# A mixture-of-experts decoder kernel: where the scatters of the routing weights stand on Pool's queue

## The chip, the core and the metric

The kernel runs on one core of one Trainium2 chip. The metric is the time of one launch on the device in microseconds. Engines are named TensorE (PE in the profile; PEld is its weight load), VectorE (DVE), ScalarE (ACT), GpSimd (POOL) and SyncE (SP). "SPq" and "POOLq" are the instructions by which an engine only issues a transfer or takes part in a barrier.

## The reference

Two decoder layers over x of 16 x 128 x 512, float32 throughout. Each has self attention, cross attention and a feed-forward part, and a layer norm after each. What matters here is the last part, a mixture of experts:

```python
logits = x @ gate_weight.T                       # 8 experts
scores = softmax(logits); topk_w, topk_idx = top_k(scores, 2)
combine = zeros((T, E)).at[arange(T)[:, None], topk_idx].add(topk_w)
gu = einsum('th,efh->tef', x, gate_up_weights)
act = silu(gu[..., :F]) * gu[..., F:]
y = einsum('tef,te,ehf->th', act, combine, down_weights)
...
y = y + (silu(sgu[:, :Fs]) * sgu[:, Fs:]) @ shared_down.T
x = layernorm(x + y)
```

T is 2048 tokens, F is 352, and the shared part that every token goes through is 704 wide.

## The kernel before

The program is a row of phases, one after the other: the attention "gqa", a latent cross attention, a ternary feed-forward part, the attentions "decay" and "causal", then the shared part of the mixture (`shared_ffn_phase`) and its experts (`expert_ffn_phase`). A phase is a block of five instruction streams, one for each engine. At its end all engines meet in a barrier, clear the phase's semaphores (L175 to L199), meet in a second one and start the next phase together.

X, the 2048 tokens by 512, stays in the on-chip memory as 16 tiles of 128 tokens. The shared phase does two things at once. TensorE multiplies the tokens by the shared weights in two halves, s = 0 and s = 1. For each group of four tiles and each of the weights' parts j it makes the products gate and up (`ups`), VectorE multiplies them (L1804, `hf`), ScalarE and VectorE split the result into a high and a low part (L1658 `hh`, L1789 `hl`), and TensorE makes the down product of it (`down`). After the last part of a group, VectorE adds the sums to that group's tiles of X (`sums`, L1783). That happens four times in each half.

Beside this the tokens are sorted by expert. VectorE works out for every token and each of its two experts a row number, `S.pos` (the last step is L1751), and the routing weight of each, `S.score`. The rows lie in 39 tiles of 128 slots in the device's memory. Pool then writes X's rows to `x_slots` (L1621: one indirect transfer for each tile t and each k of the two experts, 128 rows of 2 KB) and the routing weights to `s_slots` (L1628: 128 numbers of 4 bytes each). The expert phase loads them tile by tile: `x_slots` as input, `s_slots` as a factor at L1967.

What sets the order around the change: Pool issues in the order of its code. After every fourth tile it waits until all X scatters so far have landed (semaphore `scattered`, 16 for each). In the s = 0 half `sums` changes X, so it waits for `scattered` too: group g must have left before VectorE adds to it. TensorE's next down product that starts a bank anew waits for `sums` (`y_free`). SyncE loads three blocks of weights in this phase. The third (L1610, the first expert's) waits for VectorE's last split of the block before it (L1682), and `first_x` (L1612) waits for all of `scattered`. The scores have a semaphore of their own, `scored`; nobody but Pool waits for it, and the loads of `s_slots` come after the barrier.

```python
                if t % GT == GT - 1:
                    pool.wait_ge(scattered, 16 * 2 * (t + 1))
...
                if n and n % 2 == 0:
                    pool.wait_ge(scored, 16 * n)
...
                        if s == 0:
                            dve.wait_ge(scattered, m * (2 * 16 * 2 * GT) + (gg + 1) * 16 * 2 * GT)
```

Of the kernel before, what the change touches and what calls it, by code (L numbers as in the profile page):

```python
# [12 lines left out]
B = 16  # L13
# [143 lines left out]
class Phase:  # L157
# [11 lines left out]
    def sem(self, name):  # L169
        self.sems.append(self.ctx.enter_context(self.nc.semaphore(f"{self.name}_{name}")))  # L170
        return self.sems[-1]
# [1342 lines left out]
def shared_ffn_phase(nc, S, w):  # L1514
# [13 lines left out]
    with Phase(nc, "shared") as phase:  # L1528
# [26 lines left out]
        slots_done, rows_done, scattered, scored = sem("slots_done"), sem("rows_done"), sem("scattered"), sem("scored")  # L1555
# [46 lines left out]
        @block.sync  # L1602
        def _(sp):
            sp.dma_start(gw[:, :, :], w["router"]).then_inc(gw_in, 16)
            sp.dma_start(route[:, :], w["route"]).then_inc(route_in, 16)
            sp.dma_start(raw[:, :], w["experts"][E * P:(E + 1) * P, :]).then_inc(raw_in, 16)
            sp.wait_ge(w_lo, A_DONE)
            sp.dma_start(raw[:, :], w["experts"][(E + 1) * P:(E + 2) * P, :]).then_inc(raw_in, 16)
            sp.wait_ge(w_lo, B_DONE)
            sp.dma_start(raw[:, :], w["experts"][0:P, :]).then_inc(raw_in, 16)  # L1610
            sp.wait_ge(scattered, 16 * 2 * B)
            sp.dma_start(S.first_x[:, :], S.x_slots[0:P, :]).then_inc(first_x_in, 16)  # L1612
            sp.wait_ge(first_x_in, 16)

        @block.gpsimd
        def _(pool):
            pool.wait_ge(slots_done, 1)
            for t in range(B):
                for k in range(2):
                    at = bass.IndirectOffsetOnAxis(ap=S.pos[:, k * B + t:k * B + t + 1], axis=0)  # L1620
                    pool.indirect_dma_start(S.x_slots, at, S.X[:, t, :], None).then_inc(scattered, 16)  # L1621
                if t % GT == GT - 1:
                    pool.wait_ge(scattered, 16 * 2 * (t + 1))
            for n in range(2 * B):
                at = bass.IndirectOffsetOnAxis(ap=S.pos[:, n:n + 1], axis=0)
                if n and n % 2 == 0:
                    pool.wait_ge(scored, 16 * n)
                pool.indirect_dma_start(S.s_slots, at, S.score[:, n:n + 1], None).then_inc(scored, 16)  # L1628
            pool.wait_ge(scored, 16 * 2 * B)

        @block.scalar
# [183 lines left out]
        def _(pe):  # L1815
# [43 lines left out]
            def body(s, last):  # L1859
                for m in halves(pe, s):  # L1860
# [4 lines left out]
                    def down(q):  # L1865
                        j, r = q % J, rows_of(s, q)
                        pe.wait_ge(hl_done, t + (2 * Q * s + q + 1))
                        if s == 0 and m == 0 and q in (0, J - 1):
                            pe.wait_ge(w_lo, A_DONE if q == 0 else A_DONE + 1)


                        if j == 0 and q:
                            pe.wait_ge(y_free, m * (2 * GT) + (B * s + (q // J) * GT))
                        for i in range(GT):
                            cols = slice(i * P, (i + 1) * P)
                            for (at, high), (_, low) in zip(down_w(weh, s, j), down_w(wel, s, j)):
                                ins = products(pe, yb[i][:, at:at + high.shape[1]], hh[r, q % 2, cols], hl[r, q % 2, cols],
                                               high, low, j == 0, j == J - 1 and at + high.shape[1] == DM)
                            ins.then_inc(down_done, 1)
# [513 lines left out]
```

## Time and profile before

| | us |
|---|---|
| median of 3 runs | 2107.75 |
| lowest and highest | 2102.79, 2109.4 |
| the profiled execution | 2106.78 |
| its span in the trace | 2104.9 |

| engine | busy us | share of the span |
|---|---|---|
| PE | 1932.6 | 92% |
| PEld | 1575.4 | 75% |
| DVE | 1044.6 | 50% |
| ACT | 711.8 | 34% |
| POOL | 386.6 | 18% |

The causal attention ends at about 1550 us from the start of the span, the shared phase runs to 1791 and the expert phase to the end. A row of a timeline has the start, the length, the engine, the line, what it writes and reads, and in brackets how long the engine had stood idle and what ended that. A transfer's own row covers only its issue; "DMA to landing" counts from the start of the issue until its data is there. The granted clock is a share of TensorE's 2.4 GHz: 0.50 is 1.2 GHz.

### The profile page before, as it was taken

What the parts mean: (1) busy time and instruction counts of PE and PEld (TensorE: products, weight loads), DVE (VectorE), ACT (ScalarE), POOL (GpSimd) and SP (SyncE); (2) the same over time, 40 slices, a digit from 0 to 9 for tenths busy, and PEclk for the clock granted to TensorE, in tenths of its full rate; (3) what the DMA queues carried; (4) which work ended last, traced back from release to release, by engine and by line L of the source; (5) the groups of instructions that cost most, each with busy time, mean ns of one, the idle gap of its engine ahead of it and who ended that gap; (6) DMA issues with size and microseconds to landing.
All of it is one profiled execution on the core that took longest, in us unless ns stands there. A gap on an engine that the chain in (4) does not pass through costs nothing. (4 is left out here: it accounts for less than half of the span.)

```text
span 2104.9 us, 32789 instructions
## 1 busy us (share of the span) xinstructions
PE 1932.6 (92%) x12124; PEld 1575.4 (75%) x12124; DVE 1044.6 (50%) x1836; ACT 711.8 (34%) x2275; POOL 386.6 (18%) x339
## 2 busy tenths in 40 slices
PE   8999888999999979999899999899979996999991
PEld 6777677788888757877678877677758874899990
DVE  5676753455555455333455556676755232222224
ACT  4555634344444422212221112444632211233332
POOL 2110100000000056000021100000104222644335
PEclk9999999999999989999999999999999998999995
DMA  7211051000000021000290001000015100644257
GB/s 236 59 42 42 1 193 47 1 1 1 1 1 1 1 106 60 0 0 0 92 388 6 1 31 41 1 1 1 2 46 185 66 0 0 240 136 154 80 112 204
DMA packets 73376, 135.89 MB, mean 65 GB/s; under 512 B 13457, under 2 KB 31761, under 8 KB 71185
## 3 DMA queue, kind: packets, MB, share of 16 engines
q1 hardware_dynamic: 47376, 96.28, 13.2%
q0 software_dynamic: 7888, 27.94, 4.5%
q10 hardware_dynamic: 17968, 9.71, 1.8%
q8 instruction: 96, 1.57, 0.3%
q14 instruction: 48, 0.39, 0.1%
HBM read 90.62 MB, written 43.29 MB: 64 GB/s over the span
## 5 line engine op out<-in xcount | busy, mean ns | idle before, releaser
L1470 PE MATMUL banks<-ternary_xth,ternary_wq 128*128 (+1 forms) x352 | 141.0, 401 | 5.3 <-DVE ternary_wq L1401 3.9
L1470 PE MATMUL banks<-ternary_xtl,ternary_wq 128*128 (+1 forms) x352 | 139.4, 396 | 0.0
L571 ACT ACTIVATE causal_pr<-banks,causal_nb 128x128 f32<-128x128 f32 x256 | 89.9, 381 | 52.3 <-DVE causal_nb L713 52.3
L97 PE MATMUL banks<-latent_vh,latent_cth 128*128 128x512 f32 x256 | 104.2, 407 | 3.5 <-DVE latent_ctl L1171 3.5
L97 PE MATMUL banks<-weights,expert_xgh 128*128 x312 | 104.8, 336 | 2.4 <-DVE expert_xgl L2083 2.4
L571 ACT ACTIVATE gqa_pr<-banks,gqa_nb 128x128 f32<-128x128 f32 x256 | 89.9, 382 | 45.5 <-DVE gqa_nb L713 45.5
L99 PE MATMUL banks<-weights,expert_xgl 128*128 x312 | 101.5, 325 | 0.0
L98 PE MATMUL banks<-weights,expert_xgh 128*128 x312 | 101.5, 325 | 0.0
L99 PE MATMUL banks<-latent_vh,latent_ctl 128*128 128x512 f32 x256 | 100.2, 391 | 0.0
L98 PE MATMUL banks<-latent_vl,latent_cth 128*128 128x512 f32 x256 | 100.1, 391 | 0.0
L1430 DVE TENSOR_TENSOR ternary_hf<-ternary_sg,banks 128x512 f32<-128x512 f32 x44 | 30.2, 687 | 135.5 <-issue 79.6
L1124 ACT ACTIVATE latent_pt<-banks 128x1024 f32<-128x1024 f32 x32 | 32.9, 1027 | 187.9 <-PE banks L1270 187.9
L1371 ACT ACTIVATE ternary_sg<-banks 128x512 f32<-128x512 f32 x44 | 26.3, 598 | 192.8 <-PE banks L1470 192.8
L1115 ACT ACTIVATE latent_pr<-banks,latent_nb 128x128 f32<-128x128 f32 x256 | 90.0, 372 | 0.0
L1085 POOL TENSOR_TENSOR latent_rs<-latent_ve,mhalf 128x1 f32<-128x1 f32 x15 | 8.2, 549 | 444.3 <-DVE latent_ve L219 444.3
L97 PE MATMUL banks<-latent_xgh,latent_ch 128*128 128x256 f32 x256 | 77.2, 302 | 9.4 <-DVE latent_xgl L1165 4.6
L1470 PEld LDWEIGHTS banks<-ternary_xth,ternary_wq 128*128 128x128 f32 x352 | 67.4, 192 | 23.6 <-DVE ternary_xtl L70 4.2
L1482 PE MATMUL banks<-ternary_wq,ternary_hh 128*128 128x512 f32 x176 | 71.0, 403 | 8.1 <-DVE ternary_hl L1434 5.8
L1171 DVE TENSOR_TENSOR latent_ctl<-banks,latent_cth 128x512 fp32r<-128x512 f32 x64 | 42.8, 689 | 71.6 <-ACT latent_cth L1102 71.6
L1470 PEld LDWEIGHTS banks<-ternary_xtl,ternary_wq 128*128 128x128 f32 x352 | 67.4, 191 | 14.3
L743 DVE TENSOR_TENSOR X<-X,banks 128x512 f32<-128x512 f32 x48 | 33.0, 687 | 81.4 <-PE banks L99 81.4
L2091 DVE TENSOR_TENSOR expert_hf<-expert_sg,banks 128x352 f32<-128x352 f32 x39 | 20.3, 521 | 105.4 <-PE banks L99 105.4
(462 smaller groups left out, 5538.4 us busy)
## 6 DMA issues: line engine op xcount, KB each, us to landing
x_slots<-decay_zeros SPq DMA_DIRECT2D x39, 256.0 KB, 4.6
y_slots<-decay_zeros SPq DMA_DIRECT2D x39, 256.0 KB, 4.9
y_slots<-expert_ys SPq DMA_DIRECT2D x39, 256.0 KB, 2.1
expert_xin<-x_slots SPq DMA_DIRECT2D x38, 256.0 KB, 2.9
weights_raw<-in_expert_experts SPq DMA_DIRECT2D x4, 2176.0 KB, 9.7
gqa_tw<-in_ternary_w ACTq DMA_DIRECT2D x4, 2112.0 KB, 10.7
ternary_raw<-in_ternary_w SPq DMA_DIRECT2D x11, 768.0 KB, 4.1
expert_raw<-in_expert_experts POOLq DMA_DIRECT2D x3, 2176.0 KB, 10.0
```

The source lines that it names most:

```text
L97: pe.matmul(out, wh, xh, start=first, stop=False, **kw)
L98: pe.matmul(out, wh, xl, start=False, stop=False, **kw)
L99: return pe.matmul(out, wl, xh, start=False, stop=last, **kw)
L571: a = act.activation(pr[:, h, c, :], S.bank[2 * h + c // 4][:, (c % 4) * P:(c % 4 + 1) * P], ACT.Exp, bias=nb[:, h, c:c + 1], accum_out=su ...
L743: dve.tensor_tensor(row, row, bank, ALU.add).then_inc(free_d, 1)
L1115: a = act.activation(pr[:, c, :], S.bank[x][:, j * P:(j + 1) * P], ACT.Exp, bias=nb[:, c:c + 1], accum_out=sums[:, c:c + 1])
L1124: act.activation(pt[:, :, :], pair(1), ACT.Copy).then_inc(pt_done, 1)
L1171: dve.tensor_tensor(ctl[:, x, :], S.bank[2 + x], f32(cth[:, x, :]), ALU.subtract).then_inc(ct_lo, 1)
L1371: act.activation(sg[:, j % 2, :], gate[j % 2][:, :], ACT.Sigmoid).then_inc(sig_done, 1)
L1430: dve.tensor_tensor(hf[:, j % 2, :], sg[:, j % 2, :], up[j % 2][:, :], ALU.mult).then_inc(hf_done, 1)
L1470: a = pe.matmul(dst[:, :], wq[:, j, m, c * P:(c + 1) * P], x[:, c, toks], start=c == 0 and n == 0, stop=c == C - 1 and n == 1)
L1482: a = pe.matmul(yb[i][:, :], h[:, j % 2, i * P:(i + 1) * P], wq[:, j, 2, :], start=j == 0 and n == 0, stop=j == J - 1 and n == 1)
```

## The change

The loop over the scores is taken apart: each tile's two score scatters stand right behind that tile's two X scatters. The wait after every second score scatter is gone; there is one wait for all 32 at the end, as before. Pool's wait for the X rows after every fourth tile stays, and stands behind that tile's score scatters.

```diff
                 for k in range(2):
                     at = bass.IndirectOffsetOnAxis(ap=S.pos[:, k * B + t:k * B + t + 1], axis=0)
                     pool.indirect_dma_start(S.x_slots, at, S.X[:, t, :], None).then_inc(scattered, 16)
+                for k in range(2):
+                    n = k * B + t
+                    at = bass.IndirectOffsetOnAxis(ap=S.pos[:, n:n + 1], axis=0)
+                    pool.indirect_dma_start(S.s_slots, at, S.score[:, n:n + 1], None).then_inc(scored, 16)
                 if t % GT == GT - 1:
                     pool.wait_ge(scattered, 16 * 2 * (t + 1))
-            for n in range(2 * B):
-                at = bass.IndirectOffsetOnAxis(ap=S.pos[:, n:n + 1], axis=0)
-                if n and n % 2 == 0:
-                    pool.wait_ge(scored, 16 * n)
-                pool.indirect_dma_start(S.s_slots, at, S.score[:, n:n + 1], None).then_inc(scored, 16)
             pool.wait_ge(scored, 16 * 2 * B)
```

No other engine's instructions change. On Pool, the start of the phase (L1615 is its first instruction there), with - for before and + for now. The names in brackets are the semaphores' first users; here latent_kvr_in is `slots_done`, latent_late_chain is `scattered` and latent_late_rs is `scored`:

```order
 L1615 UNCONDITIONAL_BRANCH [waits barrier_Pool_Activation_PE_DVE_SP_gather]
 L1621 DMA x_slots<-X,pos 4992x512 [waits latent_kvr_in]
-L1621 DMA x_slots<-X,pos 4992x512 x7
+L1621 DMA x_slots<-X,pos 4992x512
+L1625 DMA s_slots<-score,pos 4992x1 x2
+L1621 DMA x_slots<-X,pos 4992x512 x2
+L1625 DMA s_slots<-score,pos 4992x1 x2
+L1621 DMA x_slots<-X,pos 4992x512 x2
+L1625 DMA s_slots<-score,pos 4992x1 x2
+L1621 DMA x_slots<-X,pos 4992x512 x2
+L1625 DMA s_slots<-score,pos 4992x1 x2
 L1621 DMA x_slots<-X,pos 4992x512 [waits latent_late_chain]
```

Tile 3's second X scatter, on which the first `sums` waits, was the 8th transfer of the phase and is the 14th.

The end of Pool's stream in this phase, before (a pair with its wait, sixteen times in all, then the wait for the last) and now:

```order
184 L1628 DMA s_slots<-score,pos 4992x1 [waits latent_late_rs]
185 L1628 DMA s_slots<-score,pos 4992x1
186 L1628 DMA s_slots<-score,pos 4992x1 [waits latent_late_rs]
187 L1628 DMA s_slots<-score,pos 4992x1
188 L1910 UNCONDITIONAL_BRANCH [waits latent_late_rs]
```

```order
179 L1625 DMA s_slots<-score,pos 4992x1 x2
180 L1621 DMA x_slots<-X,pos 4992x512 x2
181 L1625 DMA s_slots<-score,pos 4992x1 x2
182 L1621 DMA x_slots<-X,pos 4992x512 x2
183 L1625 DMA s_slots<-score,pos 4992x1 x2
184 L1909 UNCONDITIONAL_BRANCH [waits latent_late_rs,latent_late_chain]
```

The score scatters keep their number and their data; no wait stands between them any more.

## Rows read from the trace of the kernel before

**Rows 1.** The waits, 1700 to 1792: engine, line waited for, total, times, longest.
```profile
PE banks L2143 <- PEq L175: 21.3, 1, 21.3
```

**Rows 2.** The timeline of all engines, 1769.5 to 1792.2, end of the phase.
```profile
1769.17 1.37 DVE L1783 TENSOR_TENSOR X<-X,banks 128x512 f32 x2
1769.30 0.39 PE L99 MATMUL banks<-weights,shared_hl 64*128 64x512 f32 x1
...
1790.98 0.10 POOL L1990 MEMSET expert_spare<- 128x1 f32 x1 [11.27 <-POOLq L175]
...
1791.02 1.09 PE L2143 MATMUL banks<-ident,first_x 128*128 128x128 f32 x4 [21.33 <-PEq L175]
```

**Rows 3.** Line 1628: ns min/median/max, first and last start; landing times.
```profile
L1628 POOL DMA_INDIRECT s_slots<-score,pos x32: 952/957/4297, 1647.8 to 1778.8; - x32
...
DMA to landing us min/median/max: 2.5/5.9/8.5
```

**Rows 4.** Pool's timeline, 1602 to 1609.
```profile
1602.32 0.96 POOL L1621 DMA_INDIRECT x_slots<-X,pos  x1 [0.30 <-issue]
...
1607.88 2.12 POOL L1621 DMA_INDIRECT x_slots<-X,pos  x1 [0.30 <-issue]
```

**Rows 5.** The timeline of all engines, 1549 to 1552, the boundary before.
```profile
1549.41 0.55 DVE L622 TENSOR_SCALAR X<-X,causal_mv,causal_rs 128x512 f32<-128x512 f32 x1 [0.66 <-POOL causal_rs L481]
1551.84 0.33 SPq L1604 DMA_DIRECT2D shared_hf<-in_expert_router  x1
```

**Rows 6.** Line 1621: all 32, then the three issued from 1625.4.
```profile
L1621 POOL DMA_INDIRECT x_slots<-X,pos x32: 954/960/2117, 1593.1 to 1644.8; - x32
...
DMA to landing us min/median/max: 2.7/2.7/9.5
...
L1621 POOL DMA_INDIRECT x_slots<-X,pos x3: 958/961/962, 1625.4 to 1627.9; - x3
...
DMA to landing us min/median/max: 7.4/7.8/8.0
```

**Rows 7.** Line 1628: the second pair of score scatters, then the last.
```profile
L1628 POOL DMA_INDIRECT s_slots<-score,pos x2: 957/958/958, 1658.0 to 1659.2; - x2
...
DMA to landing us min/median/max: 4.7/6.0/7.2
...
L1628 POOL DMA_INDIRECT s_slots<-score,pos x2: 954/956/957, 1777.5 to 1778.8; - x2
...
DMA to landing us min/median/max: 4.9/5.2/5.4
```

**Rows 8.** VectorE's timeline, 1560 to 1700: the four sums of s = 0.
```profile
1609.68 2.47 DVE L1783 TENSOR_TENSOR X<-X,banks 128x512 f32<-128x512 f32 x4
...
1624.73 2.78 DVE L1783 TENSOR_TENSOR X<-X,banks 128x512 f32<-128x512 f32 x4 [1.15 <-PE banks L99]
...
1656.10 2.47 DVE L1783 TENSOR_TENSOR X<-X,banks 128x512 f32<-128x512 f32 x4
...
1674.05 2.78 DVE L1783 TENSOR_TENSOR X<-X,banks 128x512 f32<-128x512 f32 x4 [1.37 <-PE banks L99]
1682.82 4.69 DVE L1682 TENSOR_TENSOR weights<-weights_raw,weights 128x4352 fp32r<-128x4352 f32 x1 [5.99 <-ACT weights L1647]
```

**Rows 9.** TensorE's timeline: first instruction of three down products.
```profile
1612.30 0.47 PE L97 MATMUL banks<-weights,shared_hh 128*128 128x512 f32 x1
...
1637.53 0.39 PE L97 MATMUL banks<-weights,shared_hh 128*128 128x512 f32 x1
...
1689.56 0.65 PE L97 MATMUL banks<-weights,shared_hh 128*128 128x512 f32 x1 [2.55 <-DVE shared_hl L1789]
```

**Rows 10.** TensorE in two stretches: us, busy, PEclk, DMA share, GB/s.
```profile
1690.00:1694.00 4.00, 4.00 (x13) 0.60 0.01 0
...
1794.00:1799.00 5.00, 5.00 (x18) 0.50 0.91 297
```

**Rows 11.** SyncE's timeline, 1622 to 1624: the first expert's weights.
```profile
1623.01 0.33 SPq L1610 DMA_DIRECT2D weights_raw<-in_expert_experts  x1
```

## The prediction

> **What bounds the kernel now.** Read first the waits between 1700 us and 1792 us: TensorE, which is busy almost everywhere else, stands idle for 21.3 us at one place, ahead of the first transpose of the expert phase (L2143) [rows 1]. The timeline of that place says who is late. TensorE's last product of the shared phase starts at 1769.30, VectorE's last two additions into X run from 1769.17 to 1770.54, and then nobody works but Pool: its last two score scatters are issued at 1777.5 and 1778.8 and land 4.9 and 5.4 us later, the second at 1784.2 [rows 7], and all engines start the next phase together at 1790.98 to 1791.02 [rows 2]. A phase ends with a barrier that all engines must reach. So the end of this phase is Pool's, not TensorE's, by about 20 us. Pool is that late because of line 1628. The group of that line shows 32 scatters with a median of 0.957 us each, first start 1647.8, last 1778.8, each landing a median of 5.9 us after its issue [rows 3]: 131 us for about 31 us of issuing, the rest is the wait after every second one, that the new code doesn't have.
>
> **What is removed.** Without the waits Pool's own work is 64 issues. Their pitch is 1.26 us (from the first, 1593.1, to the eighth, 1602.32, are 9.2 us, less 0.4 us for a slow start, so 8.8 over seven steps) [rows 4, 6]. 64 x 1.26 = 81 us, to 1674; with the waits for rows that are counted below, some ten microseconds more, about 1685. The last score lands at most 8.5 us later [rows 3], so before 1694. That is 76 us ahead of VectorE's last addition: all that Pool still has at the end is hidden by the s = 1 half of TensorE's products (L97 to L99), and if that cover were shorter by 76 us, Pool would be the end again.
>
> What ends the phase then? VectorE at 1770.54. The price of a boundary whose last work is VectorE's is read at the one before this phase: the last addition there runs from 1549.41 for 0.55, and SyncE's first issue of the next phase is at 1551.84 [rows 5]: 1.88 us. With it the expert phase starts at 1770.54 + 1.88 = 1772.4 and not 1790.98, a gain of **18.6 us** if nothing in the shared phase moves. It takes in the 6.8 us between the last score's landing (1784.2) and 1790.98, of which 1.9 are the boundary and 4.9 are something that follows Pool's own last scatter; Pool would now have that 70 us early, so I count all of it.
>
> **What is moved, and what waits for it.** X is scattered from the same rows that VectorE adds into later (sums, L1783), so sums waits for `scattered`, four tiles at a time, and TensorE's next down product waits for sums (y_free). Putting two score scatters behind each tile doubles the distance between tiles. Four times it can matter:
>
> Group 1 (tiles 0 to 3). The last X scatter was the 8th issue, 1602.32; it is now the 14th: 6 x 1.26 = 7.6 us later, 1609.9. One issue of that stretch, at 1607.88, took 2.12 us instead of 0.96 [rows 4]; I keep these 1.2 us, since it falls in the same time: 1611.1. An X scatter alone lands after 2.7 us [rows 6], so 1613.8. But the score scatters of tile 2 were issued just before. Those of the second pair landed after 4.7 and 7.2 us (issued 1658.0 and 1659.2) and those of the last after 4.9 and 5.4 [rows 7]. If X's count must come in behind them it is 1614 to 1616. I take 1615. sums began at 1609.68 with four additions in 2.47 us, and TensorE's down product that reads their bank began at 1612.30, right after [rows 8, 9]. Here is no slack: 1615 + 2.5 + 0.15 = 1617.7, a stall of **5.4** us (4.0 if X lands after its 2.7).
> A stall has a second price. After the 2.55 us of idle at 1689.56 the granted clock was 0.60 over 1690 to 1694 [rows 9, 10]: one stretch of about 3.4 us at 1.2 instead of 2.4 GHz, 1.7 us lost. I add **1.7** once. The shift is now 7.1.
>
> Group 2 (tiles 4 to 7). Pool's 17th issue starts at 1593.1 + 16 x 1.26 + 1.6 = 1614.9, a little after X has landed, so about 1615.3; tile 7's second X scatter is 13 issues on, 1631.7, with half a microsecond for another slow issue 1632. In the kernel before it was issued at 1627.9, beside the load of a whole expert's weights that SyncE issued at 1623.01, and the three last ones needed 7.4 to 8.0 us to land [rows 6, 11]. That load waits for VectorE's line 1682, which is now behind the late sums, so it moves along by the same 5 us and still covers 1632. Landing at 1640. sums (2.8) to 1642.8, then hf, ACT's hh and hl of about 0.7 each: 1645.0. Before, sums stood at 1624.73 and TensorE's down product at 1637.53; sums, hf, hh and hl need 5.0 us of that, so there was some 8 us of room [rows 8, 9]. TensorE goes on at 1645.0 instead of 1637.53: a shift of 7.5, **0.4** more than it brings along.
>
> Groups 3 and 4. Pool goes on at 1640.3, tile 11's rows are issued by 1656.7 and land by 1663; sums needs them at 1656.10 + 7.5 = 1663.6. Tile 15's: 17th issue after that at 1660.6, so 1677.1 and 1683; needed at 1674.05 + 7.5 = 1681.6, and behind that sums VectorE had 5.99 us of idle before line 1682 [rows 8]. Both fit: **0**.
>
> **The queue itself** is what the trace can't show, since no X scatter stands behind a score scatter in it. From one side: no cost beyond a single landing (X after 2.7). From the other: score scatters are served one behind the other. In the two pairs of [rows 7] the second landed 3.8 and 1.8 us after the first, though issued 1.3 apart, so a scatter may hold the queue for 1.8 to 3.8 us, with a middle of 2.8, and a tile for 5.6, against 5.05 us of issuing. That is near enough to even that I count only the short delay above.
> The Trainium skill, DMA: Bandwidth & Descriptors, Queues, rings and completion order, says that a transfer's semaphore count is a strongly ordered write that lands only after every earlier write of the same DMA engine. By that rule X always lands behind the scores ahead of it; no row here shows it. By it the stall in group 1 would be near its 1616 end, without it near 1613.8.
>
> **Clock behind the boundary.** Before, the granted clock was 0.50 over 1794 to 1799 although TensorE was busy for all 5.00 us [rows 10]. The idle time ahead is now under 3 us and not 21. Between nothing and half of those 5 us comes back; I take **0.9**.
>
> **Sum.** 18.6 - 5.4 - 1.7 - 0.4 + 0.9 = 12.0 us. The profiled execution took 2106.78 (span 2104.9), so 2094.8; on the median of the runs, 2107.75, it is **2095.8**. The load of the weights, the tiles of x_slots and Pool's work of the expert phase all start from the boundary and move with it.
>
> **Rivals.** (a) X doesn't queue behind scores: stall 4.0 in group 1, tile 7 after 2.7 us and so no second stall, 18.6 - 4.0 - (0 to 1.7) + 0.9 = 14 to 15.5, about 2093. For it: an X scatter's landing is flat at 2.7 us wherever nothing large is under way. Against it: scores land more slowly than X, though they carry 4 bytes a row and X 2 KB. Chance 0.17.
> (b) **Slower: the queue is the limit.** Served strictly in turn, a tile costs two scores at 2.8 to 3.8 and two X scatters of about 0.7. Tile 15's rows land at 1593 + 4 + 15 x pace. They are needed at 1674 + 6; the gain of 18.6 is gone when they land after 1698.6, so the point is a pace of **6.8** us a tile. At 5.6 + 1.4 = 7.0 it is about 3 us slower than before; at 3.3 a scatter (8.0 a tile) tile 15 lands at 1717, TensorE ends 37 us late, and the time is 2107.75 + 18.4 = 2126. Of this speaks for it that the pair takes 8.65 us from issue to issue (129.7 us over 15 pairs, from 1647.8 to 1777.5) [rows 3, 7]; against it that a part of that is plain latency, which overlaps. Slower by over 0.3%: 0.08.
> The Trainium skill, same page, Specifications, says that transfers under 512 bytes are done by read-modify-write; it would make (b) likelier, since every score is 4 bytes. The trace agrees so far as 5.9 us against 2.7 go.
> (c) Between: some queueing, two or three stalls, a shift of 13 to 24 us where I have 7.5. Gain from 6 down to a loss of 5, 2102 to 2112, most of it within 0.3%. Chance 0.17 with the mild half of (b).
> (d) Pool's tail of 4.9 us is a price of the boundary and not of Pool's last scatter: gain 7 us, 2101. The boundary of [rows 5] speaks against it. Chance 0.05.
>
> **Chances.** 0.3% (6.3 us) is about what a measurement can tell from no change. Forecast 0.53 (gain 8 to 15), (a) 0.17, (d) 0.05, (c) 0.17, (b) 0.08. Faster by over 0.3%: 0.53 + 0.17 + some of (d) = 0.73; within 0.3%: 0.19; slower 0.08. The range goes from (a) with no stall at all (2107.75 - 18.6 - 1.5 = 2087.6) to no gain, 2107.
>
> **What the profile of after would show.** TensorE's wait at L2143 down from 21.3 to under 3 us; Pool's last issue before 1700; all starts at about 1780. X scatters with a median landing above 2.7 us if they queue. In sums one wait for x_slots of about 5 us at 1610 and one at 1632. It would be wrong if Pool's issues of group 4 run far past 1685, which is (b), or if TensorE has no idle near 1612, which is (a) or better.

## The result, and the profile after

| | before | after |
|---|---|---|
| median us | 2106.11 (4 runs) | 2125.07 (4 runs) |
| lowest and highest | 2102.79, 2109.4 | 2121.66, 2127.38 |
| the profiled execution | 2106.78 | 2123.46 |
| its span | 2104.9 | 2121.7 |

The changed kernel is **slower**: 1.0079 times the time of before, 95% interval 1.0061 to 1.0097. The forecast was 2095.8 us, and its range ended at 2107.0.

In this execution the sort gave Pool its row numbers 2.1 us later than in the one of before (Pool's first issue at 1595.2 instead of 1593.1 [rows 6]); every time below holds these 2.1 us.

The end of the phase, in the waits between 1750 and 1812 (engine, line, total, times, longest), and in the timeline. The row of L2142 answers to the wait of [rows 1], all three of the timeline to [rows 2]:

```profile
POOL expert_spare L1989 <- POOLq L175: 105.6, 1, 105.6
```
```profile
1805.96 0.39 PE L99 MATMUL banks<-weights,shared_hl 64*128 64x512 f32 x1
1808.50 0.10 POOL L1989 MEMSET expert_spare<- 128x1 f32 x1 [105.56 <-POOLq L175]
1808.54 1.08 PE L2142 MATMUL banks<-ident,first_x 128*128 128x128 f32 x4 [2.19 <-PEq L175]
```

The wait of 21.3 us is gone: TensorE stands idle for 2.19 us between the phases, and Pool is there 105 us ahead. But the expert phase starts at 1808.50, where it started at 1790.98. TensorE's last product, at 1769.30 before, comes at 1805.96.

Where TensorE lost that is plain from two windows, from the sort's end to TensorE's last product of the phase, of before and then of after (stretch, its length, busy us and matmuls, granted clock, share of the DMA engines, GB/s):

```profile
1593.00:1769.70 176.70, 173.63 (x793) 0.99 0.17 62
```
```profile
1595.10:1806.30 211.20, 181.34 (x793) 0.92 0.25 52
```

The same 793 matmuls take 34.5 us longer: 26.8 us more idle time (29.9 against 3.1) and 7.7 us more busy time, at a clock of 0.92 instead of 0.99 (the mean over the stretch, stalls included). Against that stand 19.1 us from the boundary (21.33 to 2.19). With the start 2.1 us later this is the 17.5 us by which the expert phase starts late.

The waits of after between 1597 and 1720 say who was waited for:

```profile
DVE X L1782 <- DMA x_slots<-X,pos: 29.5, 2, 18.9
DVE shared_hf L1803 <- remote: 24.7, 2, 13.8
POOL x_slots L1621 <- DMA x_slots<-X,pos: 24.3, 3, 13.9
...
PE banks L97 <- DVE X L1782: 10.3, 1, 10.3
```

and VectorE's timeline shows the four `sums` (L1782 now; [rows 8] before) and the third place at which TensorE stood:

```profile
1622.12 2.48 DVE L1782 TENSOR_TENSOR X<-X,banks 128x512 f32<-128x512 f32 x4 [10.62 <-DMA x_slots<-X,pos]
1657.62 2.48 DVE L1782 TENSOR_TENSOR X<-X,banks 128x512 f32<-128x512 f32 x4 [18.92 <-DMA x_slots<-X,pos]
1683.58 2.47 DVE L1782 TENSOR_TENSOR X<-X,banks 128x512 f32<-128x512 f32 x4
1705.80 0.69 DVE L1803 TENSOR_TENSOR shared_hf<-shared_sg,banks 128x512 f32<-128x512 f32 x1 [13.79 <-remote]
1709.69 0.69 DVE L1782 TENSOR_TENSOR X<-X,banks 128x512 f32<-128x512 f32 x1 [1.81 <-PE banks L99]
```

TensorE's down products behind these, which answer to [rows 9]:

```profile
1624.75 0.77 PE L97 MATMUL banks<-weights,shared_hh 128*128 128x512 f32 x1 [10.25 <-DVE X L1782]
1662.14 0.80 PE L97 MATMUL banks<-weights,shared_hh 128*128 128x512 f32 x1 [9.34 <-DVE shared_hl L1788]
1707.93 0.58 PE L97 MATMUL banks<-weights,shared_hh 128*128 128x256 f32 x1 [7.22 <-DVE shared_hl L1788]
```

Three stalls, 26.8 us. Each is followed by a stretch at half clock (PEclk is the third number from the end, in front of the DMA share and GB/s):

```profile
1624.70:1630.40 5.70, 5.65 (x13) 4.47 (x14) 2.60 (x3) 0.63 (x1) 4.29 (x5) 0.50 0.25 92
1662.00:1668.00 6.00, 5.86 (x14) 4.60 (x15) 1.38 (x3) 0.63 (x1) 4.76 (x5) 0.50 0.30 89
1707.90:1712.30 4.40, 4.37 (x20) 4.37 (x21) 1.50 (x3) 0.00 (x0) 0.00 (x0) 0.50 0.26 42
```

Half of 5.65, 5.86 and 4.37 is 7.9 us: the busy time that was added (7.7) to within 0.2.

Why the rows are late is on Pool's queue. The last X scatter of group 1 and the first one behind the wait for that group, then the same of group 2, in the timeline of Pool:

```profile
1613.30 0.96 POOL L1621 DMA_INDIRECT x_slots<-X,pos  x1 [0.30 <-issue]
...
1622.37 0.95 POOL L1621 DMA_INDIRECT x_slots<-X,pos  x1 [5.58 <-DMA x_slots<-X,pos]
...
1640.50 0.96 POOL L1621 DMA_INDIRECT x_slots<-X,pos  x1 [0.30 <-issue]
...
1657.87 0.95 POOL L1621 DMA_INDIRECT x_slots<-X,pos  x1 [13.88 <-DMA x_slots<-X,pos]
```

Tile 3's rows are there 8.8 us after their issue (sums starts at 1622.12), tile 7's 17.1 us. Beside it runs the load of the first expert's weights, which answers to [rows 11]; line 1610 of after:

```profile
L1610 SPq DMA_DIRECT2D weights_raw<-in_expert_experts x1: 327/327/327, 1638.1 to 1638.1; - x1
...
DMA to landing us min/median/max: 18.2/18.2/18.2
```

It took 10.2 us before, and the rows issued beside it needed some 8 us then [rows 6], not 2.7. Single landings of the scatters themselves are mostly missing from this trace, so those of [rows 3, 6, 7] have no counterpart in it; the times above are those at which the waiting engines went on.

### The profile page after: what moved, and what is told of

Its sections match the earlier page's. It is cut to its first block and busy times, and to the rows that moved or that the text cites. A ratio compares the mean times of both kernels' runs of the same rounds, so it can differ in the third digit from the quotient of the medians.

```text
span 2121.7 us, 32790 instructions
## 1 busy us (share of the span) xinstructions
PE 1941.6 (92%) x12124; PEld 1583.6 (75%) x12124; DVE 1043.1 (49%) x1836; ACT 711.6 (34%) x2275; POOL 384.6 (18%) x339
## 5 line engine op out<-in xcount | busy, mean ns | idle before, releaser
L98 PE MATMUL banks<-latent_xgl,latent_ch 128*128 128x256 f32 x256 | 72.9, 285 | 0.0
L99 PE MATMUL banks<-latent_xgh,latent_cl 128*128 128x256 f32 x256 | 72.8, 285 | 0.0
```

The costliest lines, as they stand in the source:

```text
L98: pe.matmul(out, wh, xl, start=False, stop=False, **kw)
L99: return pe.matmul(out, wl, xh, start=False, stop=last, **kw)
```

## Does the boundary give what was expected?

Every ratio from here on is to the kernel before, run beside the kernel in question, and the brackets give its 95% interval. Two kernels leave the boundary's gain alone in view. The first keeps the order of before and takes only the waits between the scores away; the second is the changed kernel with its four lines of score scatters and their wait left out (the experts are then weighted by the zeroed slots).

```diff
             for n in range(2 * B):
                 at = bass.IndirectOffsetOnAxis(ap=S.pos[:, n:n + 1], axis=0)
-                if n and n % 2 == 0:
-                    pool.wait_ge(scored, 16 * n)
                 pool.indirect_dma_start(S.s_slots, at, S.score[:, n:n + 1], None).then_inc(scored, 16)
```

> The kernel before with one part of the change alone: the waits after every second score scatter are gone, but all 32 X scatters still stand first. Theory Q (X's counts land behind the scores ahead of them in the queue, a score scatter holds it about 2.8 us): no score is ahead of an X scatter, so the four sums start where they did (the first some 17 us after Pool's first scatter), Pool's last issue is near 1690, the last landing near 1740, and the shared phase ends with VectorE: 18.6 us less than before, about 2088. Rival R (a backlog of small writes delays TensorE's own signals, as at 1698 in the changed kernel, wherever it stands): the backlog of 90 us lies beside TensorE's work and costs stalls of several microseconds each, 2095 to 2110.

> The changed kernel without the 32 score scatters and their wait; the routing weights stay zero, so the experts' part of the output is left out, while the expert phase does the same work. Every theory: X scatters as in the kernel before, no stall, the phase ends with VectorE, about 2088. It measures the term of 18.6 us for the end of the phase by itself; if the tail of 4.9 us belongs to the boundary, 2093.

Measured: rows first without waits **2087.06** us (4 runs; ratio 0.9897, 0.9876 to 0.9919), without scores 2086.91 (4 runs; 0.9892, 0.9875 to 0.9909). The last product and the start of the next phase with the rows first, from the timeline, and its group of score scatters:

```profile
1769.29 0.38 PE L99 MATMUL banks<-weights,shared_hl 64*128 64x512 f32 x1
...
1771.83 0.10 POOL L1988 MEMSET expert_spare<- 128x1 f32 x1 [79.56 <-POOLq L175]
```
```profile
L1626 POOL DMA_INDIRECT s_slots<-score,pos x32: 954/958/5002, 1647.8 to 1691.1; - x32
...
DMA to landing us min/median/max: 5.0/7.0/9.3
```

TensorE ends where it did before (1769.30), and the next phase starts 19.1 us earlier than at 1790.98. So the removal of the waits is worth its 18.6 us, and the move of the scores is what costs. The group shows more: 32 scatters issued without a pause in 43 us land at most 9.3 us behind their issue, so they don't pile up; they are served at one in 1.4 us or less. A scatter that held it for the 2.8 us of the prediction would have left the last one some 45 us behind.

Whether the order among the scores matters (tile by tile, as the changed kernel has them, and not all of k = 0 first) was one kernel more:

```diff
-            for n in range(2 * B):
+            for m in range(2 * B):
+                n = (m % 2) * B + m // 2
```

> As the kernel with all X scatters first and no waits between the scores, but the scores go tile by tile (both experts of a tile, then the next tile), the order that they have in the changed kernel. Theory M (scores and X scatters hinder each other when mixed): the order among the scores does nothing, the last issue is near 1692 and the landings have a median of 6 to 9 us, as with the other order. Theory O (a tile's two score scatters meet at the same addresses, so this order is slow by itself): landings of 10 us and more, 32 scores need 2.7 us each, the last landing near 1735. Either way about 2088.

2087.95 us (one run), landings 4.5/6.9/9.5. It doesn't matter.

## What the score scatters do to the rows

All kernels of this section have the order of the changed one. In the first the score scatters carry rows of 2 KB to `y_slots` instead (the experts' weights are again the zeroed ones). In the second the score slots lie 256 bytes apart, and the loads read them with that stride:

```diff
-                    pool.indirect_dma_start(S.s_slots, at, S.score[:, n:n + 1], None).then_inc(scored, 16)
+                    pool.indirect_dma_start(S.y_slots, at, f32(xtl[:, 0, 0:DM]), None).then_inc(scored, 16)
```
```diff
-                    at = bass.IndirectOffsetOnAxis(ap=S.pos[:, n:n + 1], axis=0)
-                    pool.indirect_dma_start(S.s_slots, at, S.score[:, n:n + 1], None).then_inc(scored, 16)
+                    at = bass.IndirectOffsetOnAxis(ap=spos[:, n:n + 1], axis=0)
+                    pool.indirect_dma_start(S.s_slots.rearrange("a (b c) -> (a b) c", c=1), at, S.score[:, n:n + 1], None).then_inc(scored, 16)
...
+                dve.tensor_scalar(spos[:, :], posf[:, :, :].rearrange("p k t -> p (k t)"), float(64), None, ALU.mult).then_inc(slots_done, 1)
...
-        S.s_slots = nc.dram_tensor("s_slots", (SLOTS, 1), F32).ap()
+        S.s_slots = nc.dram_tensor("s_slots", (SLOTS, 64), F32).ap()
```

`spos` are the row numbers times the distance between slots, counted in numbers of 4 bytes.

> The changed kernel with each score scatter replaced by a scatter of 128 rows of 2 KB (from a tile that nobody changes, into y_slots, which is overwritten later), at the same place and with the same semaphore; the routing weights stay zero, so the experts' part of the output is left out. Theory Q: it is the 4-byte writes that hold the queue, so X lands 2.7 to 4 us after its issue, the first sums starts about 4 us late instead of 10, and the time is 2090 to 2096. Rival (the number and the place of the scatters, not their kind): X lands after 9 to 17 us and the time stays near 2125.

> The changed kernel with s_slots widened from 4 bytes a slot to 256, so that no two scores fall into the same 256 bytes; same scatters, same 4 bytes each, same order. VectorE makes a second list of row numbers (one more small instruction). Theory Q1 (writes of 4 bytes are slow because neighbours in memory take turns): a score scatter lands after 3 us, X after 3 to 4, time 2090 to 2096. Theory Q2 (each 4-byte write is slow wherever it goes): X lands as late as in the changed kernel and the time stays at 2120 to 2128.

Measured: 2099.39 us with 2 KB rows (4 runs; 0.9953, 0.9936 to 0.997), 2096.36 with the spread slots (4 runs; 0.9942, 0.9923 to 0.9962). The spread kernel's first two sums, its X scatters, and its score scatters:

```profile
1613.53 2.48 DVE L1787 TENSOR_TENSOR X<-X,banks 128x512 f32<-128x512 f32 x4 [4.53 <-DMA x_slots<-X,pos]
1639.68 2.48 DVE L1787 TENSOR_TENSOR X<-X,banks 128x512 f32<-128x512 f32 x4 [9.94 <-DMA x_slots<-X,pos]
```
```profile
L1625 POOL DMA_INDIRECT x_slots<-X,pos x32: 956/960/1232, 1592.7 to 1676.9; - x32
...
DMA to landing us min/median/max: 2.7/2.7/6.9
```
```profile
L1629 POOL DMA_INDIRECT s_slots<-score,shared_spos x32: 954/958/2292, 1595.5 to 1679.4; - x32
...
DMA to landing us min/median/max: 2.1/2.1/8.7
```

The spread kernel is what was forecast for the changed one, in its time and in its places: sums waits 4.5 us in group 1 and TensorE 4.2 us behind it, the rest is hidden. It has the same number of transfers, of the same 4 bytes, in the same order, and is 28.7 us faster. With 2 KB rows the time lies 3.4 us above what was expected (2090 to 2096), but far from the 2125 of the rival. So neither the number of small scatters nor their place on the queue makes the loss, but that the numbers are written next to one another: row numbers are given out expert by expert in the order of the tokens, so the 128 numbers of a scatter fall on a few short runs of neighbouring slots. Scatters of 512 times the data hurt far less, if they go to rows of their own. Why neighbouring writes are slow, no run here shows.

How far apart must the slots be? Three kernels keep the order and the waits of before and only send the scores into an array of their own, with 8192, 8448, 16 and 64 bytes from slot to slot (it isn't read; the experts are weighted by zeros). The one with 16 bytes:

```diff
-                at = bass.IndirectOffsetOnAxis(ap=S.pos[:, n:n + 1], axis=0)
+                at = bass.IndirectOffsetOnAxis(ap=spos[:, n:n + 1], axis=0)
...
-                pool.indirect_dma_start(S.s_slots, at, S.score[:, n:n + 1], None).then_inc(scored, 16)
+                pool.indirect_dma_start(S.s_wide, at, S.score[:, n:n + 1], None).then_inc(scored, 16)
...
+                dve.tensor_scalar(spos[:, :], posf[:, :, :].rearrange("p k t -> p (k t)"), float(4), None, ALU.mult).then_inc(slots_done, 1)
```

In the kernel before Pool waits 92.9 us for them, 15 times.

> The kernel before, with its waits, but the scores are scattered into a wide array at a distance of 8192 bytes from slot to slot, which nobody reads; s_slots stays zero, so the experts' part of the output is left out. Theory C (the memory takes the small writes of one channel in turn, and channels change every 256 bytes and repeat every 8192): all 128 writes of a scatter fall on one channel, about 0.09 us each, a pair takes some 23 us instead of 6.5, and the time grows by some 250 us. Theory N (only neighbours within the same 256 bytes take turns): a pair takes about 3 us and the time falls to about 2090.

> The same with a distance of 8448 bytes (8192 + 256) between slots; the experts' part of the output is left out in the same way. Theory C: neighbours now fall on different channels, a scatter lands after about 3 us, and the time is about 2090. If this is as slow as 8192, it is the wide distance as such that costs.

> As with the wide array and the waits of the kernel before, but at a distance of 16 bytes from slot to slot; the array is read by nobody, s_slots stays zero, so the experts' part of the output is left out. With 4 bytes a score scatter landed after a median of 5.9 us, with 8192 after 2.1. If writes take turns within the same 64 bytes, 16 neighbours become 4 and the landing falls to 3 us or less; if within the same 256 or 512 bytes, it falls to some 3.5 to 4.5 us.

> The same at a distance of 64 bytes, the experts' part of the output left out in the same way. Turns within 64 bytes: 2.1 us, as at 8192. Turns within 256 or 512 bytes: 4 or 8 neighbours are left and the landing is 2.3 to 3.0 us.

The waits of Pool on line 1629 at 8192, 16 and 64 bytes:

```profile
  DMA s_wide<-score,shared_spos: 22.2, 15
```
```profile
  DMA s_wide<-score,shared_spos: 26.2, 15
```
```profile
  DMA s_wide<-score,shared_spos: 22.5, 15
```

At 8448 bytes it is 22.2 too. The median landing is 2.1 us at 8192 and at 8448 bytes; at 16 and 64 the landings are missing from the traces, and the waits stand for them. The times are 2091.36, 2087.07, 2087.05 and 2092.74 us, one run each (in the first and the last the phase itself began 4.6 and 6.3 us later, before the first scatter, so that isn't the scores'). The theory that places which repeat at 8 KB share a part of the memory falls: 8192 is as good as 8448. 16 bytes do nearly all of it; less than 16 was not tried. In the changed kernel itself 16 bytes are enough as well:

> The changed kernel whose score slots lie 16 bytes apart (an array 4 times as large, of which each first number is used; the scores' loads read it with that stride), all else as in the changed kernel. Theory N (what hurts is scores that are written next to one another, and 16 bytes are distance enough): 2094 to 2099 us as with 256 bytes apart (2096.36), X rows landing 3 to 7 us after issue. Rival (the distance has to be more than a line of 64 bytes when rows are mixed in, or it was the 256 bytes' zeroing or loads that shifted things): 2110 us or more.

2097.38 us (7 runs; 0.9951, 0.9934 to 0.9968), sums waits 15.5 us in two places, X scatters land after 2.7/2.8/7.9, the scores after 2.1/2.2/8.8.

## Does the loss come through the wait of sums?

The changed kernel with X scatters that send a fixed tile (so x_slots holds other data) and with sums not waiting for them:

```diff
-                    pool.indirect_dma_start(S.x_slots, at, S.X[:, t, :], None).then_inc(scattered, 16)
+                    pool.indirect_dma_start(S.x_slots, at, f32(xtl[:, 0, 0:DM]), None).then_inc(scattered, 16)
...
-                        if s == 0:
-                            dve.wait_ge(scattered, m * (2 * 16 * 2 * GT) + (gg + 1) * 16 * 2 * GT)
```

> The changed kernel, but the X scatters take their rows from a tile that nobody changes (so x_slots holds other rows and the experts' part of the output is wrong in value, not in work), and VectorE's sums no longer waits for them. Theory L (all of the loss is sums waiting for X's landing): no stall is left, about 2088. Theory S (TensorE's own completion signals also come late while the queue is full, as the product that ended near 1698 and was seen at 1705.8 suggests): one or more stalls of 2 to 8 us stay beside the scatters, 2092 to 2105, and VectorE or ScalarE show waits on signals and not on x_slots.

2088.99 us (4 runs; 0.9923, 0.9899 to 0.9948), 36 us less than the changed kernel. Its rows of L1625, and Pool's wait for the rows:

```profile
DMA to landing us min/median/max: 4.7/7.9/12.9
```
```profile
POOL x_slots L1621 <- DMA x_slots<-shared_xtl,pos: 17.6, 3, 6.8
```

The scores land as late as ever and Pool still waits for rows (it goes on 10.9 us behind the issue of tile 3's last and 10.6 behind tile 7's), but nobody else does. So the first two stalls go through that wait. The third, which was no wait for rows, isn't in this trace either: TensorE waits 2.8 us in all before its products, as in the kernel before. That the same wait brings it about isn't shown by that. A smaller step is to keep the scores out of each group's rows only, eight rows, the wait, then the eight scores of that group:

```diff
                     pool.wait_ge(scattered, 16 * 2 * (t + 1))
+                    for u in range(t + 1 - GT, t + 1):
+                        for k in range(2):
+                            n = k * B + u
+                            at = bass.IndirectOffsetOnAxis(ap=S.pos[:, n:n + 1], axis=0)
+                            pool.indirect_dma_start(S.s_slots, at, S.score[:, n:n + 1], None).then_inc(scored, 16)
```

> Between the two orders: eight X scatters of four tiles, the wait for them, then these tiles' eight score scatters without waits, and so on. It tests the room that I read before each sums. Group 1 has no score ahead, so its sums starts at its old place. Tile 7's second X scatter is the 24th issue, some 32 us after the first, and stands behind eight scores: landing after 7 to 10 us, near 1635 on the old time scale, where sums stood at 1624.7 with 8 us of room and the clock at full speed: a stall of 0 to 4 us. Groups 3 and 4 fit. 2088 to 2093; if the room isn't there, 2096 and more.

2098.15 us (10 runs; 0.996, 0.9946 to 0.9974, from 2093.68 to 2107.86), above the 2088 to 2093 that were expected. Better than the changed kernel, 11 us behind the one with all rows first. The profiled execution is the slowest of the ten, 2107.86. VectorE's wait of group 2 and a later one in it:

```profile
1640.05 2.48 DVE L1783 TENSOR_TENSOR X<-X,banks 128x512 f32<-128x512 f32 x4 [13.45 <-DMA x_slots<-X,pos]
...
1686.98 0.69 DVE L1804 TENSOR_TENSOR shared_hf<-shared_sg,banks 128x512 f32<-128x512 f32 x1 [13.62 <-remote]
```

Group 1's sums is on time. Group 2's waits 13.45 us, since its rows start behind eight slow scores and fall on the weights' load, and 3.88 of that reach TensorE, within the 0 to 4 expected. The larger stall is the second, 7.05 us of TensorE. It is no wait for rows, and it stands at the same product as the third stall of the changed kernel; the next section is about it. What share of the 11 us each has in the other nine executions, one trace can't tell.

## TensorE's own lateness

The third stall of the changed kernel is not for rows. VectorE's product at 1705.80 needs ScalarE's part, there since 1699.2, and TensorE's up product, whose last matmul the trace has at 1697.61; it went on 8.2 us later, and the profile says "remote": it has no record of what released it. The kernel by groups shows the same at the same product: last matmul at 1678.95, VectorE at 1686.98, 8.0 us later. To see such a thing by itself, the kernel with rows first got two probes amid its slow scores: one scatter of 2 KB rows behind the tenth, and SyncE's load of `first_x` at the 21st.

```diff
                 pool.indirect_dma_start(S.s_slots, at, S.score[:, n:n + 1], None).then_inc(scored, 16)
+                if n == 9:
+                    pool.indirect_dma_start(S.y_slots, at, f32(xtl[:, 0, 0:DM]), None).then_inc(probed, 16)
+                if n == 20:
+                    pool.memset(mark[:, :], 0.0).then_inc(go, 1)
+            pool.wait_ge(probed, 16)
...
+            sp.wait_ge(go, 1)
             sp.dma_start(S.first_x[:, :], S.x_slots[0:P, :]).then_inc(first_x_in, 16)
```

> All X scatters first, no waits between the scores, and two probes among the scores: behind the tenth a scatter of 128 rows of 2 KB by Pool into y_slots (which is overwritten later), and behind the 21st SyncE's load of first_x, 256 KB, from another queue. Alone such a scatter lands after 2.7 us and that load after 2.5. Theory L (a transfer's count lands behind the small writes ahead of it, in its own queue and in others): the scatter needs 6 to 10 us and the load 5 to 10 us. Rival (the small writes are slow in themselves and hinder nobody): both stay under 3.5 us, and the late X rows of the changed kernel have another cause. The time is near 2088 either way.

One run, 2114.44 us, 27 over the kernel without probes, where about 2088 was expected. TensorE, which starts a matmul every 0.23 us, started 17 in the 28.8 us behind 1668.19, up to 3.5 us apart. From its timeline:

```profile
1668.19 0.39 PE L99 MATMUL banks<-weights 128*128 128x512 f32 x1
1670.30 0.39 PE L97 MATMUL banks<-weights 128*128 128x512 f32 x1 [1.72 <-issue]
...
1682.28 0.59 PE L97 MATMUL banks<-weights 128*128 128x512 f32 x1 [2.21 <-issue]
1683.68 0.59 PE L98 MATMUL banks<-shared_xtl,weights 128*128 128x512 f32 x1 [0.82 <-issue]
1686.48 0.59 PE L99 MATMUL banks<-weights 128*128 128x512 f32 x1 [2.21 <-issue]
```

"Issue" is idle time in which it waited for nothing that the profile shows. Is it the scatter or the load, does it come back, and does it need the slow scores?

> The kernel of the best order (rows first, then the 32 scores without waits between them, 2087.06 us) with only the first of the two probes left: one extra scatter of 2 KB rows (to y_slots, whose contents are written over later) on Pool behind the tenth score. With both probes TensorE ran from 1668.4 us on at one matmul in 1.4 to 3.5 us for some 28 us and the time was 2114.44. Theory S1 (a scatter of 2 KB rows among slow scores is what makes TensorE late): 2108 to 2118 us, with TensorE slowed within 10 us of the extra scatter's issue. Theory S2 (it was the SyncE load; the slowing before its issue is something else): 2086 to 2092 us.

> The kernel of the best order (2087.06 us) with only the second of the two probes left: SyncE's load of first_x is issued when Pool has reached the 21st score (about 1678 us) and not before the scores. Theory S1 (the 2 KB scatter did it): 2086 to 2090 us, the load landing some 5 to 15 us after its issue with nobody waiting for it. Theory S2 (the load did it): 2105 us or more, TensorE slowed behind 1678.

> The kernel with both probes (2114.44 us in the one execution so far), once more and in several executions. Each probe alone gave 2086.99 and 2091.72. Theory B (the two together reliably slow TensorE's stream of instructions): 2108 to 2120 us in most executions, with TensorE at one matmul in over 1 us for more than 15 us behind 1668. Theory R (a disturbance that comes in some executions of any kernel that mixes large transfers among slow scores, and not in others): a spread between 2087 and 2115 us, median under 2095.

> Both probes, with the scores scattered to places 16 bytes apart in an array of their own (which the second stage doesn't read: its scores are the zeroed ones; no work goes away). Theories B and R agree that without slow scores nothing happens: 2085 to 2090 us, highest execution under 2093. If TensorE is slowed here too, it isn't the scores that are written next to one another.

The scatter alone 2086.99 and the load alone 2091.72 (one run each), both together once more 2090.89 (4 runs, 2090.14 to 2091.92; 0.9924, 0.9901 to 0.9946), both with spread scores 2091.83 (4 runs; 0.9928, 0.9906 to 0.995). So neither probe alone brings the slowing back, and the load alone is no 2105 us or more. The slowing came in one of five executions of the same program, so it isn't the probes' steady price, and **this part stays open**. The probes did show a steady thing: amid the slow scores the 2 KB scatter landed after 8.6 us (the one of the scatter probe alone) and the load of `first_x` after 9.6 (the load alone) and 10.7 (both, where the scatter took 9.4); amid spread scores 2.8 and 3.5. In the kernel before that load took 2.5 us.

## The prediction, step by step

- **The boundary, 18.6 us: right.** 19.1 in the changed kernel and with rows first. That Pool's last 4.9 us belong to Pool's own late scatter and not to the boundary, which rival (d) doubted, holds.
- **Pool's issues in group 1: right.** Tile 3's last scatter was forecast for 1611.1, and for 1613.2 with this execution's later start; it was at 1613.30, one slow issue of 2.31 us among them.
- **Its landing: the step that failed.** "An X scatter alone lands after 2.7 us", and 3.9 behind scores: it took 8.8. The stall is 10.25 us instead of 5.4, and the half clock behind it costs 2.8 instead of 1.7. What the text took from the rows was how an X scatter lands among its own kind; among scores on neighbouring slots it lands as late as they do, and these are slow because they are neighbours.
- **Group 2: failed by the same term.** Issued at 1640.50, landing forecast 8 us later beside the weights' load, measured 17.1; that load took 18.2 us instead of 10.2. The 8 us of room that was to hide it were right (spread slots: sums waits 9.94 and TensorE none for it); what came in was too late for them. Tile 7's issue at 1640.50 instead of 1634.1 (1632 and the late start) is mostly that too: Pool had waited for group 1's rows. A stall of 9.34 us and 2.9 of clock, where 0.4 stood.
- **Group 4: nothing was foreseen.** Pool's waits for the rows grew to 24.3 us and pushed its last X scatter to 1699.46 instead of 1677; but the stall of 7.22 us there, with 2.2 of clock, came by TensorE's late signal, and its cause is open: 9.4 of the 26.5 us between the gain forecast (12.0) and the loss that the measured terms add up to (14.5, below). Tile 15's rows were there by 1705.54, when SyncE's load of `first_x` goes out that waits for all of them, so within 6.1 us of their issue.
- **"The queue itself": failed, in both directions.** The two pairs of [rows 7] gave a holding of 1.8 to 3.8 us, from which I found issue and service about even and counted "only the short delay". As a rate it was too slow: unthrottled scores take 1.4 us or less. As a delay for others it was too small. The rows were read as one scatter holding up the next; with rows first 32 of them land 5.0 to 9.3 us after their issue and still don't fall behind, so such landings overlap and give no rate. [Rows 3] and [rows 6] held the warning, 5.9 us for 4 bytes a row against 2.7 for 2 KB, and the text weighed it for rival (b) alone.
- **Rival (b)** names the right side. That it names nearly the right time (2126) is luck: it belongs to a pace of 8.0 us a tile, and the pace was 6.85 (from tile 0's second X scatter, 1596.8, to tile 15's, 1699.46), at which its own working gives a time about 1 us above that of before. Its mechanism, a queue that serves 2.8 to 3.8 us a scatter, isn't what happened; the pace came from Pool's waits for rows that were late, and the time was lost in groups 1 and 2 and behind the late signal, and by the clock.
- **The clock behind the boundary, 0.9: right.** From the start of the expert phase half clock lasts to 1814.7, which is 6.2 us with TensorE busy for 4.54, where it was 8.0 with 6.36 (1791.0 to 1799.0): 0.9 us come back.

The sum with the measured terms: 19.1 - 26.8 (idle) - 7.7 (clock) + 0.9 = -14.5, so 14.5 us lost; with the 2.1 us by which this execution's phase began late, 16.6. The two profiled executions differ by 16.7.

The skill's rule that was weighed against the trace (the Trainium skill, DMA: Bandwidth & Descriptors, Queues, rings and completion order: a semaphore's count lands only after every earlier write of that DMA engine) fits what was measured: a 2 KB scatter that lands after 2.7 us by itself and 2.8 amid spread scores needs 8.6 amid slow ones, as long as these need themselves. The trace agrees as far as that goes; no run separates the count from the data. Its figure of 512 bytes (same page, Specifications), below which a transfer is done by read-modify-write, doesn't tell the two kinds of scores apart: all are of 4 bytes, and land after 2.1 us with distance and 5.9 without.

## What to carry to other kernels

Small scatters that nobody waits for belong behind those that somebody waits for, and then need no throttle between them: rows first, scores unthrottled is 2087.06 us, 1.0% under the kernel before and 1.8% under the changed one, and no kernel that leaves nothing out is clearly faster. Before moving transfers together, compare their landings by size: where 4 bytes land later than 2 KB, what stands behind them inherits that time. And where numbers that are scattered one by one stand among transfers that somebody waits for, give them 16 bytes each, if what reads them can bear the stride: 2097.38 us instead of 2125.07 in the order of the changed kernel. With the rows first it gained nothing (with both probes 2091.83 spread, 2090.89 not).

## What the runs showed of the hardware

- Scatters of 128 single numbers to neighbouring slots land after a median of 5.9 us; with slots 16, 256, 8192 or 8448 bytes apart, 2.1 to 2.2 us (at 64 bytes only Pool's waits are known, and they are as short). It isn't the size alone, nor places that repeat at 8 KB.
- While such scatters are under way, others pay with them: X rows 8.8 us instead of 2.7, and 17.1 instead of some 8 beside the load of the weights, that load itself 18.2 instead of 10.2 (9.4 amid spread scores), a load of 256 KB 9.6 instead of 2.5.
- In the changed kernel and in the one by groups TensorE's signal came 8 us after its matmul, and in one of five executions of the kernel with both probes its stream of matmuls ran at 17 in 28.8 us. None of the seven traces with spread slots shows either, and neither do seven of the ten with neighbouring ones. Why, is open.
